# Second layer's attention on a Trainium2 core: both heads of a pair side by side in the array, scores two units ahead

## What is computed

```
latent_kv = x @ w_kv_down
kv = latent_kv @ w_kv_up
k, v = (kv[..., :HD], kv[..., HD:])
q = (x @ w_q).reshape(Bx, Tx, N_HEAD, HEAD_SIZE)
att = jnp.einsum('bqhd,bkhd->bhqk', q, k) * scale
att = jnp.where(causal, att, -jnp.inf)
att = jax.nn.softmax(att, axis=-1)
y = jnp.einsum('bhqk,bkhd->bqhd', att, v)
return y.reshape(Bx, Tx, HD) @ w_out
```

## Time and profile before

| | |
|---|---|
| runs | 2755.13, 2746.61, 2756.91 us; median 2755.13 us |
| profiled execution | span 2757.3 us from the first to the last instruction |
| busy: PE | 2420.2 us (88%) |
| busy: PE weight loads | 1810.4 us (66%) |
| busy: DVE, ACT, POOL | 1575.1, 1082.8, 523.8 us (57, 39, 19%) |
| the stage of this change | 1634.5 to 2435.5 us, and project_out to 2467 us |
| granted TensorE clock, mean | 0.934 of full speed |

### The profile page before, as it was taken

How to read it: one execution, slowest core, us unless ns; L and a number is a source line. 1 busy time by engine, 2 the same in 40 slices (tenths; PEclk the granted TensorE clock), 3 DMA queues, 4 the chain that set the end, 5 groups by cost and what they waited for, 6 DMA issues and landing times. The chain is left out here.

```text
span 2757.3 us, 49484 instructions
## 1 busy us (share of the span) xinstructions
PE 2420.2 (88%) x18575; PEld 1810.4 (66%) x18575; DVE 1575.1 (57%) x3695; ACT 1082.8 (39%) x3096; POOL 523.8 (19%) x993
## 2 busy tenths in 40 slices
PE   4887998978989799898995879999999999978997
PEld 3776776767767677677774555556556556666765
DVE  6566675657656676566764755545545545533334
ACT  2544444434444344443442234434434434421112
POOL 5321333223322233223331000000000000000000
PEclk9999999999989899998997889989989989988999
DMA  3000000000000000000001000000000000010000
GB/s 130 1 2 1 1 1 2 1 1 1 1 1 1 1 1 1 2 1 2 1 1 55 0 0 1 1 2 1 1 2 1 1 2 1 1 62 1 1 0 15
DMA packets 5258, 20.96 MB, mean 8 GB/s; under 512 B 1848, under 2 KB 1984, under 8 KB 4032
## 3 DMA queue, kind: packets, MB, share of 16 engines
q1 hardware_dynamic: 5056, 17.95, 1.7%
HBM read 16.90 MB, written 1.05 MB: 7 GB/s over the span
## 5 line engine op out<-in xcount | busy, mean ns | idle before, releaser
L1443 DVE TENSOR_REDUCE b_nmax<-ps 128x1 f32<-128x1024 f32 (+7 forms) x256 | 194.0, 758 | 325.5 <-PE ps L1343 324.7
L817 DVE TENSOR_TENSOR prod<-ps,mt 128x128 f32<-128x128 f32 x512 | 147.2, 287 | 386.6 <-PE ps L687 257.5
L1339 PE MATMUL ps<-b_kT,b_qT 64*128 64x512 f32 (+3 forms) x768 | 328.1, 535 | 16.9 <-issue 15.4
L1410 ACT ACTIVATE b_prob<-ps,b_nmax 128x1024 f32<-128x1024 f32 (+7 forms) x256 | 189.6, 740 | 343.0 <-DVE b_nmax L1443 342.9
L322 PE MATMUL ps<-xT,taps 128*128 (+1 forms) x2176 | 303.7, 282 | 0.0
L322 PEld LDWEIGHTS ps<-xT,taps 128*128 128x128 f32 x2176 | 265.9, 191 | 11.6
L560 POOL COPY last<-di 128x512 f32<-128x512 f32 x130 | 81.1, 635 | 685.8 <-PE ps L548 484.2
L1339 PEld LDWEIGHTS ps<-b_kT,b_qT 64*128 64x128 f32 x768 | 127.4, 191 | 119.6 <-issue 102.8
L1072 PE MATMUL ps<-xTn,f_w 128*128 x352 | 168.4, 614 | 24.9 <-PEq L981 18.5
L1086 PEld LDWEIGHTS ps<-f_w,f_hT 128*128 128x128 f32 x1408 | 167.6, 193 | 31.6 <-issue 24.0
L1456 DVE COPY b_probT<-ps 128x512 f32<-128x512 f32 (+3 forms) x256 | 150.1, 586 | 63.1 <-PE ps L1365 61.3
(11 more groups left out here) (211 smaller groups left out, 4564.7 us busy)
## 6 DMA issues: line engine op xcount, KB each, us to landing
wtap<-in_taps SPq DMA_DIRECT2D x4, 1024.0 KB, 11.1
f_w<-in_f_w SPq DMA_DIRECT2D x2, 2048.0 KB
f_w<-in_f_w SPq DMA_DIRECT2D x2, 768.0 KB, 5.7
xT<-in_xT SPq DMA_DIRECT2D x2, 512.0 KB, 13.8
stream<-in_x_tok SPq DMA_DIRECT2D x1, 1024.0 KB, 12.0
wkv<-in_w_kv_up SPq DMA_DIRECT2D x1, 1024.0 KB, 8.4
out<-stream SPq DMA_DIRECT2D x4, 256.0 KB, 2.5
wraw<-in_WvT SPq DMA_DIRECT2D x1, 512.0 KB, 6.1
```

The source lines that it names most:

```text
L817: ch.step(nc.vector.tensor_tensor(prod[:, b, :, :, :], zi, mtc[:, :, b, NB * c + i, :, :], ALU.mult))
L1339: mm = pe.matmul(bank[:, 0:c1 - c0], lhsT=qT[rows, f, b * T + i * P:b * T + (i + 1) * P], rhs=kT[rows, f, b * T + c0:b * T + c1], start=Tr ...
L1410: nc.scalar.activation(prob[:, u % 2, 0:n], src, ACT.Exp, bias=nmax[:, u % 4:u % 4 + 1], accum_out=total[:, w % 4, h:h + 1]).then_inc(sems ...
L1443: nc.vector.tensor_reduce(nmax[:, u % 4:u % 4 + 1], src, axis=AX.X, op=ALU.max, negate=True).then_inc(sems["max_done"], 1)
```

## The change

The stage is written anew; the table of units and their order within a sequence stay.

- **Projection apart.** There is no hardware loop: the pairs come in two groups of four (`GP = 4`), each with a block of 48 projections of 512 columns (16 each of q, k and v; copied out by ACT and DVE in turn) and then a block of attention with 64 units. q goes to yT, where the unit's result later replaces it. POOL has nothing to do in the stage.
- **Scores of both heads together.** `scores(w, part)` takes 256 columns of head 0 (array rows 0 to 63) and then of head 1 (rows 64 to 127), into different banks; the mask is added for both at the end. Long units have banks 0 to 3, short ones banks 4 and 5. The list starts with the scores of units 0 and 1; those of unit w + 2 are issued behind the first transposes of unit w, all in one run (`early = 1`).
- **Transposes in chunks of four.** The 2n tiles of both heads and the spread reciprocal are one row of 2n + 1 tiles, turned four at a time into bank 6, the only bank for it. ACT copies out chunks 0, 2 and 4 of long units, DVE the others and all of short ones.
- **Values of the unit before** are cut into shares that lie behind the chunks.
- **Reciprocal.** DVE's RECIPROCAL reads the 128 x 2 sums broadcast and writes 128 x 128 in one instruction; PE turns it as the last tile.
- `project_out` issues each product as two halves of 64 output rows, one per sequence.

The diff, cut to its core:

```diff
@@ -1190,14 +1190,13 @@
 AH, AD = 16, 64
 NP = AH // 2
 TT = T // P
+GP = 4
...
-        pair_w = sb("pair_w", [P, 2, 3, P])
-        qT, kT = sb("qT", [P, 2, B * T]), sb("kT", [P, 2, B * T])
-        v = sb("v", [P, 2, NT, P])
-        prob = sb("prob", [P, 2, T])
-        probT = sb("probT", [P, 4, TT, P])
-        nmax, total, inv = sb("nmax", [P, 4]), sb("total", [P, 4, 2]), sb("inv", [P, 4, 2])
-        spread = sb("spread", [P, 2, 2, AD])
-        recipT = sb("recipT", [P, 2, P])
+        kT = sb("kT", [P, GP, B * T])
+        v = sb("v", [P, GP, B * TT, P])
+        prob = (sb("prob_long", [P, 2, T]), sb("prob_short", [P, 2, T // 2]))
+        probT = (sb("probT_long", [P, 2 * TT + 1, P]), sb("probT_short", [P, TT + 1, P]))
+        nmax, total, inv = sb("nmax", [P, 8]), sb("total", [P, 4, 2]), sb("inv", [P, 2, 2, AD])
...
+        units = [(m, b, i) for m in range(GP) for b in range(B) for i in order]
...
+        def chunks(w):
+            return (2 * tiles(w) + 1 + 3) // 4
+        first_chunk = [sum(chunks(x) for x in range(w)) for w in range(W + 1)]
+        by_scalar = [not short(w) and c % 2 == 0 for w in range(W) for c in range(chunks(w))]
...
+        def span_of(w, c):
+            return 4 * c, min(4 * c + 4, 2 * tiles(w) + 1)
+        PIECES = [("q", m, s) for m in range(GP) for s in range(4)] + [("k", m, s) for m in range(GP) for s in range(4)]
+        PIECES += [("v", n, 0) for n in range(B * TT)]
...
+        for grp in range(NP // GP):
...
-                    scores(0)
-                    for u in range(U + 1):
-                        if u + 1 < U:
-                            scores(u + 1)
-                        if u in at_step:
-                            piece(u)
-                        if u < U:
-                            turn(u)
-                        if u >= 2 and u % 2 == 0:
...
+            def scores_of(w, h):
+                if short(w):
+                    return ps[:, 4 + h, 0:tiles(w) * P]
+                return ps[:, 2 * h:2 * h + 2, :].rearrange("p k e -> p (k e)")[:, 0:tiles(w) * P]
...
+                    def scores(w, part):
+                        m, b, i = units[w]
+                        if part == 0 and w >= 2:
+                            pe.wait_ge(exp_done, 2 * (w - 2) + 2)
+                        c0, c1 = 256 * part, min(256 * part + 256, tiles(w) * P)
+                        last = c1 == tiles(w) * P
+                        for h in range(2):
+                            rows = slice(AD * h, AD * h + AD)
+                            mm = pe.matmul(scores_of(w, h)[:, c0:c1], lhsT=yT[rows, GP * grp + m, b * T + i * P:b * T + (i + 1) * P],
+                                           rhs=kT[rows, m, b * T + c0:b * T + c1], start=True, stop=not last,
+                                           skip_group_check=True)
+                        if last:
+                            for h in range(2):
+                                mm = pe.matmul(scores_of(w, h)[:, c1 - P:c1], lhsT=cst["ident16"][:, :],
+                                               rhs=cst["above_diag"][:, :], start=False, stop=True, skip_group_check=True)
+                            mm.then_inc(s_done, 1)
+                    def turn(w, c):
+                        n, g = tiles(w), first_chunk[w] + c
+                        lo, hi = span_of(w, c)
+                        pe.wait_ge(exp_done, 2 * w + (1 if hi <= n else 2))
+                        if g >= 1:
+                            by_act, count = kept_by(g - 1)
+                            pe.wait_ge(t_kept_a if by_act else t_kept_v, count)
+                        for t in range(lo, hi):
+                            out = ps[:, 6, (t - lo) * P:(t - lo + 1) * P]
+                            if t < 2 * n:
+                                mm = pe.transpose(out, prob[short(w)][:, t // n, (t % n) * P:(t % n + 1) * P], cst["ident"][:, :])
+                            else:
+                                pe.wait_ge(recip_done, w + 1)
+                                mm = pe.transpose(out, inv[:, w % 2, :, :].rearrange("p h c -> p (h c)"), cst["ident"][:, :])
+                        mm.then_inc(t_done, 1)
+                    def values(w, j):
+                        m, b, i = units[w]
+                        n = tiles(w)
+                        if j == 0:
+                            a, d = through(w)
+                            pe.wait_ge(t_kept_v, d)
+                            if a:
+                                pe.wait_ge(t_kept_a, a)
+                            if w >= 1:
+                                pe.wait_ge(y_done, w)
+                        for h in range(2):
+                            cols = slice(AD * h, AD * h + AD)
+                            mm = pe.matmul(ps[cols, 7, 0:P], lhsT=v[:, m, b * TT + j, cols], rhs=probT[short(w)][:, h * n + j, :],
+                                           start=(j == 0), stop=(j == n - 1), skip_group_check=True)
+                        if j == n - 1:
+                            mm.then_inc(o_done, 1)
+                    for w in range(2):
+                        for part in range(score_parts(w)):
+                            scores(w, part)
+                    for w in range(W + 1):
+                        ahead = score_parts(w + 2) if w + 2 < W else 0
+                        behind = tiles(w - 1) if w >= 1 else 0
+                        turns = chunks(w) if w < W else 1
+                        for c in range(turns):
+                            if w < W:
+                                turn(w, c)
+                            early = 1
+                            if c < early:
+                                for part in range(ahead * c // early, ahead * (c + 1) // early):
+                                    scores(w + 2, part)
+                            late = turns - early + 1
+                            if c >= early - 1:
+                                for j in range(behind * (c - early + 1) // late, behind * (c - early + 2) // late):
+                                    values(w - 1, j)
+                    def exponent(w, h):
+                        act.wait_ge(max_done, 2 * w + h + 1)
+                        if w >= 2:
+                            act.wait_ge(t_done, first_chunk[w - 1])
+                        nc.scalar.activation(prob[short(w)][:, h, 0:tiles(w) * P], scores_of(w, h), ACT.Exp,
+                                             bias=nmax[:, (2 * w + h) % 8:(2 * w + h) % 8 + 1],
+                                             accum_out=total[:, w % 4, h:h + 1]).then_inc(exp_done, 1)
+                    def keep_turned(w, c):
+                        act.wait_ge(t_done, first_chunk[w] + c + 1)
+                        if w >= 2:
+                            act.wait_ge(y_done, w - 1)
+                        lo, hi = span_of(w, c)
+                        nc.scalar.copy(probT[short(w)][:, lo:hi, :], ps[:, 6, 0:(hi - lo) * P].rearrange(
+                            "p (j t) -> p j t", j=hi - lo)).then_inc(t_kept_a, 1)
+                    for h in range(2):
+                        exponent(0, h)
+                    for w in range(W):
+                        mine = [c for c in range(chunks(w)) if by_scalar[first_chunk[w] + c]]
+                        for c in mine[:1]:
+                            keep_turned(w, c)
+                        if w + 1 < W:
+                            exponent(w + 1, 0)
+                        for c in mine[1:2]:
+                            keep_turned(w, c)
+                        if w + 1 < W:
+                            exponent(w + 1, 1)
+                        for c in mine[2:]:
+                            keep_turned(w, c)
+                @block.vector
+                def _(dve):
+                    def row_max(w, h):
+                        dve.wait_ge(s_done, w + 1)
+                        k = (2 * w + h) % 8
+                        nc.vector.tensor_reduce(nmax[:, k:k + 1], scores_of(w, h), axis=AX.X, op=ALU.max, negate=True).then_inc(
+                            max_done, 1)
+                    def keep_turned(w, c):
+                        dve.wait_ge(t_done, first_chunk[w] + c + 1)
+                        if w >= 2 and c <= 1:
+                            dve.wait_ge(y_done, w - 1)
+                        lo, hi = span_of(w, c)
+                        nc.vector.tensor_copy(probT[short(w)][:, lo:hi, :], ps[:, 6, 0:(hi - lo) * P].rearrange(
+                            "p (j t) -> p j t", j=hi - lo)).then_inc(t_kept_v, 1)
+                    def divide(w):
+                        m, b, i = units[w]
+                        dve.wait_ge(o_done, w + 1)
+                        nc.vector.tensor_tensor(yT[:, GP * grp + m, b * T + i * P:b * T + (i + 1) * P], ps[:, 7, 0:P],
+                                                probT[short(w)][:, 2 * tiles(w), :], ALU.mult).then_inc(y_done, 1)
+                    for w in range(2):
+                        for h in range(2):
```

(28 more changed lines are left out.)

291 lines of the change are left out of this document (74 added, 217 removed).

## The result

The changed kernel takes 2769.86 us in the median of four runs (2767.28 to 2772.82), the kernel before 2750.87 (four runs on the same chip, 2745.32 to 2756.91). The ratio is 1.0073 with a 95% interval of 1.0053 to 1.0093: **slower by 0.7%**, 7 us above the forecast of 2763 and inside its range. The change itself was missed by more: from median to median it is +19 us, where +8 was forecast. The profiled execution has a span of 2765.3 us, where the sum said 2765. That looks better than it is. The sum started from a profiled execution of the kernel before whose span, 2757.3, lies above all four of its runs, and the one profiled here is the fastest of its four; and inside the sum terms were off and cancelled.

What follows compares the result with a forecast made beforehand. PE was taken as the bound, busy 776 of the stage's 801 us. Slots 703, fill 8, projections 91.5 and block ends 6 summed to 808.5, +8: span 2765, median 2763 us, range 2712 to 2845 (forecast's own 2743 to 2783).

Steps and rivals of the forecast that it cites:

- Scores: Attention slots: both row halves work at once, a tile costs 0.22 us instead of 0.43, 124 us less on PE.
- rival A: Scores: the row halves do not overlap, 0.22 us a tile more, +104 us, 2867; chance 0.12.
- the penalty of 0.2 for an odd number of tiles: Scores: weight loads make a last part of 128 columns cost 0.43 us, not 0.22, in slots issuing odd tiles.
- Transposes in chunks of four: Attention slots: with one bank, a chunk costs 1.40 us with DVE's copy and 1.30 with ACT's; PE works 0.44.
- Reciprocal: DVE's 128 x 128 reciprocal takes 1.05 us, bounds 0.27 and 1.2; PE's chunk with it waits behind it.
- The slots: Attention: eight slots, one for each unit length, sum to 43.95 us; 16 times that is 703 us.
- rival C: Attention: waits overlap better, reciprocal nearer 0.27 us (30 us) and DVE operations overlapping (10 more), 2723; chance 0.30.
- rival B: Attention: PE's idle time puts 15% at the half clock level, +53 us, 2816; chance 0.15.
- the likeliest case: Whole kernel: PE work is taken away and returned as waits, 2763 us, from 2743 to 2783; chance 0.43.
- Rest: Stage outside the slots: fill 8 us, projections 91.5, block ends and starts 6; the loop's three turns go.
- project_out in halves: project_out: 512 half records at 0.055 us replace 256 at 0.11, gaining nothing.
- POOL's empty list: Stage: POOL's copies, 44.5 us, go with nothing gained; the 0.3 us in PE's chain was hidden by scores.

Runs made afterwards that it cites:

- serial: Changed kernel with all scores of head 0 issued ahead of all of head 1; one run, 2818.64 us, stage 57.6 us longer.
- narrow: Changed kernel with the reciprocal taken as 128 x 2 on DVE and spread by a POOL copy; one run, 2731.14 us, stage 38.2 us shorter.
- the two fillers: Changed kernel plus useless PE products in slots of 8 and 7 tiles, the second with more in slots of 8 and 1: 2756.66 and 2739.4 us.

## Why the prediction was right, and where terms cancelled

*Scores.* Right in the main: four records in 0.43, and rival A falls. The Trainium skill (TensorE: Matmul & The Clock Gate, Part 3) says that tiles of different row groups run at once; the trace agrees, 0.109 us from record to record. Wrong was the penalty of 0.2 for an odd number of tiles: from the first score record to the mask it is 1.93, 1.72, 1.50, 1.28, 1.07 us for 8, 7, 6, 5, 4 tiles, steps of 0.21 or 0.22 throughout. Weight loads did not bound the pairs. Rival A's price was too high, as `serial` shows.

*Transposes in chunks of four.* Right in kind, 0.09 short in size. The slot of 7, where nothing stands between the chunks:

```profile
1742.38 0.61 PE L1353 MATMUL ps<-ident,b_prob_long 128*128 128x128 f32 x4
1743.03 0.69 DVE L1441 COPY b_probT_long<-ps 128x512 f32<-128x512 f32 x1 [1.58 <-PE ps L1353]
...
1743.87 0.63 PE L1353 MATMUL ps<-ident,b_prob_long 128*128 128x128 f32 x4 [0.88 <-DVE b_probT_long L1441]
1744.53 0.58 ACT L1410 COPY b_probT_long<-ps 128x512 f32<-128x512 f32 x1 [2.61 <-PE ps L1353]
...
1745.26 0.52 PE L1353 MATMUL ps<-ident,b_prob_long 128*128 128x128 f32 x2 [0.77 <-ACT b_probT_long L1410]
```

The chunks start 1.49 (DVE) and 1.39 us (ACT) apart, where 1.40 and 1.30 were laid: PE follows 0.15 after the copy's end and not 0.05. The slots of 8, 7, 6 and 5 were met within 0.11 us all the same, since the scores in their first cycle were priced too high (slot of 8: 2.43 to the second chunk, not 2.7).

*Reciprocal.* Predicted 1.05, measured 0.943: the slope is nearer 6.3 ns an element than 7.0 (788 ns over 126 elements). The estimate by the Trainium skill (VectorE: DVE Perf Modes, section "First, the fixed hardware budget") was 1.2, and the measurement decides against it.

*The slots.* Predicted 43.95, measured 42.14 at full clock. All of the difference is in the short slots (1: -0.68, 4: -0.64, 2: -0.48, 3: -0.17). In the slot of 1 the prediction had 1.75 us until the reciprocal's transpose. The slot begins at 1779.24, so it is 1.27, of which PE idles 0.85:

```profile
1779.51 0.94 DVE L1456 RECIPROCAL b_inv<-b_total 128x128 f32<-128x128 f32 x1
...
1780.51 0.33 PE L1356 MATMUL ps<-ident,b_inv 128*128 128x128 f32 x1 [0.85 <-DVE b_inv L1456]
```

The scores and values behind it take 3.0 us instead of 3.2. This term was 29 us too long, in the direction of rival C and not far from its 40. But C had most of that from a reciprocal of 0.27 us; it was 0.11 below the 1.05, worth 5 us in three slots. The rest is handoffs, scores and DVE's starts in the short slots laid too long, and no run separates them.

*What the sum left out* is rival B. It priced 15% of the attention at the half level with 53 us. Measured are 95.6 us of half level in the slots of the two blocks, 13% of 712, and they cost (44.48 - 42.14) x 16 = **37 us**; less than a half of the slowed time, and least where PE waits (0.21 us for 1.30 in a slot of 7). So these two errors, -29 and +37, nearly cancelled; the likeliest case had a time near the measured one and an incomplete mechanism, and that is luck. It should have been "C in part and B in part". The argument used against B, that PE busy for 4.1 of 5 us kept its clock in layer 0, was true of that row, but here the shares inside a slot are uneven, and the stretch of two bare chunk cycles is busy for only 1.76 of 3.40 us. I read a mean, and the falls stand behind single stretches.

*Rest.* The stage with the latent was forecast at 808.5 and took 820.9. The two blocks of attention took 362.1 and 363.0 us instead of about 355: the two errors above, 8 together, and 6 more for filling and draining. The projections and block ends took 2 less. (In the sum for them, 96 x 0.43 gives 41.3 a group; the factor of 2 counts the groups, and the total of 91.5 holds.) That the span still came out at 2765.3 is luck once more, outside the stage: it begins 6.2 us earlier than in the kernel before (1628.3 for 1634.6), in layers that did not change, and behind its end the span is 316.1 us where it was 321.8, with 43 us at the half level instead of 52. project_out in halves was rightly costed at nothing: from its first record to its last it was 31.3 us before (the earlier trace rows is the busy time) and is 29.2 after, but it began with 5.6 us at the half level before and with 2.8 after. POOL's empty list was rightly said to gain nothing, and the empty engine is what `narrow` used.

*Where the expected gain went.* PE is busy for 90 us less in the stage. Its idle time there rose by 110 us, from 25 to 135. And with 47 us more at the half level, part of the work that is left runs slower. Take the half level out, at the 0.39 us for each that the slots show (37/95.6) up to 0.5: the stage before would be 764 to 771 us and the one after 760 to 772. This is an estimate, and for the kernel before no run stands behind it. By it the two lists are worth the same at full clock, and the 20 us that were lost are the clock's; the two fillers, which move nothing but the clock, agree. Why the 90 us gained nothing is the waits.

## What to carry to other kernels

When work leaves the bound engine but its waits stay, look at the stretches of the list in which it idles most, not at its mean: here they cost twice, once as idle time and again as a slower clock behind them. Cover each wait with work that was to be issued anyway, and check that what is moved had not covered a longer wait elsewhere: the same edit gained 42 us in the long slots alone and lost 23 when applied to all. With a single execution, compare the stage that the edit touches and not the total, and begin it at the same instruction in both kernels.

## What the runs showed of the hardware

- In the steady part of the blocks the granted clock fell to the half level (1.2 GHz) for 3.4 or 6.8 us at a time, behind stretches such as the one shown, with PE busy for about half of it (1.76 us of 3.40 there) and no single idle time of over 1 us. 20 us of useless products took away 42 us of the half level.
- At the half level a slot lengthens by 0.2 to 0.5 us per us: 1.48 for 3.35 in the slot of 2, where PE never waits, and 0.21 for 1.30 in a slot of 7 with its two waits.
- The untouched layers ahead of the stage differ by up to 18 us between executions, together with their own time at the half level.
- A RECIPROCAL of 128 x 128 takes 943 ns, of 128 x 2 155 ns.
